# Two-layer graph attention on one core: layer-0 probabilities turned by VectorE in 32x32 blocks over a DRAM scratch, with every engine's order rewritten

## The reference

```python
# layer 0, per graph; H = 8 heads of hd = 64
Q, K, V = x @ W_q + b_q, x @ W_k + b_k, x @ W_v + b_v
scores = einsum('bihd,bjhd->bhij', Q, K) / sqrt(hd)
scores = scores + (x @ w_g[:D])[:, :, None] + (x @ w_g[D:])[:, None, :] + b_g + log(adj + 1e-9)
x1 = einsum('bhij,bjhd->bihd', softmax(scores), V) + x
# layer 1, per graph; one head of 512
q, k = x1 @ Wq + bq, x1 @ Wk + bk
attn = where(adj == 0, 0, softmax(where(adj == 0, -1e18, q @ k.T / sqrt(512))))
out = layernorm(x1 + (attn @ x1) @ Wc) * gamma + beta
```

## Time and profile before

| | |
|---|---|
| median of 3 runs | 2469.9 us (2468.51 to 2470.04) |
| the profiled execution, its own time | 2468.04 us |
| its span, first to last instruction | 2466.3 us |
| share of the span busy | PE 98%, DVE 72%, ACT 52%, POOL 31% |
| DMA | 119.36 MB, 13.5% of 16 engines' span |
| one step | 74.78 us |

### The profile page before, as it was taken

One profiled execution on the slowest core, in us unless ns is written; L12 is line 12 of the kernel. 1 busy time (PEld: TensorE's weight loads), 2 busy tenths in 40 slices (PEclk: granted clock), 3 DMA queues, 4 the chain that ended last, 5 costly groups with the idle time before them and its releaser, 6 DMA issues.

```text
span 2466.3 us, 40779 instructions
## 1 busy us (share of the span) xinstructions
PE 2425.6 (98%) x14544; PEld 2003.8 (81%) x14544; DVE 1777.0 (72%) x5600; ACT 1278.4 (52%) x3602; POOL 774.0 (31%) x1022
## 2 busy tenths in 40 slices
PE   7999999999999999999999999999999999999995
PEld 5888888888888888888888888888888888888884
DVE  4667777767777777777677777687777777776766
ACT  4455445555455555455554455554555554555542
POOL 0133223332323332333332233323233323234322
PEclk9999999999999999999999999999999999999998
DMA  5010111110111101111101111101111111111000
GB/s 197 31 56 22 56 48 47 54 50 29 56 48 44 56 30 48 48 56 44 56 22 56 48 54 46 56 23 56 48 44 56 35 44 52 52 43 57 27 14 26
DMA packets 63179, 119.36 MB, mean 48 GB/s; under 512 B 6272, under 2 KB 22784, under 8 KB 58752
## 3 DMA queue, kind: packets, MB, share of 16 engines
q1 hardware_dynamic: 62976, 116.75, 13.5%
HBM read 83.17 MB, written 33.55 MB: 47 GB/s over the span
## 4 chain that ended last, share of the span: by engine, by line
PE 96%; DVE 1%; SPq 1%; ACT 1%; DMA 0%; issue 0%; POOL 0%; DVEq 0%
PE bank L199 25%; PE bank L201 24%; PE bank L200 24%; PE bank L383 6%; PE bank L404 5%; PE bank L540 5%; PE bank L393 5%; PE bank L319 1%; PE bank L502 1%; PE bank L584 1%; DVE x1n L935 0%; DMA x1n<-in_wkT 0%; ACT probs L680 0%; PE bank L341 0%; PE bank L329 0%
## 5 line engine op out<-in xcount | busy, mean ns | idle before, releaser
L1122 POOL TENSOR_TENSOR probs<-probs,rcp 128x512 f32<-128x512 f32 x256 | 297.3, 1182 | 1105.5 <-DVE rcp L887 1105.5
L680 ACT ACTIVATE probs<-probs,nmax 128x128 f32<-128x128 f32 x1024 | 397.0, 389 | 144.2 <-DVE nmax L877 144.2
L935 DVE STREAM_TRANSPOSE x1n<-x1T 32x512 f32<-32x512 f32 x512 | 359.6, 702 | 8.1 <-DMA out<-x1n 1.6
L877 DVE CUSTOM_DVE_ANT_0 probs<-bank,bias 128x128 f32<-128x128 f32 x1024 | 226.9, 286 | 40.0 <-issue 40.0
L857 DVE TENSOR_TENSOR v_sb<-bank,bv_b 128x512 f32<-128x512 f32 x128 | 87.8, 687 | 229.6 <-PE bank L404 172.9
L706 ACT ACTIVATE g_sb<-bank,consts 128x512 f32<-128x512 f32 x128 | 88.1, 688 | 309.8 <-PE bank L201 308.0
L199 PE MATMUL bank<-x_hi,wk_hi 128*128 128x512 f32 x512 | 209.2, 409 | 8.6 <-DVE x_lo L818 8.6
L199 PE MATMUL bank<-wv_hi,x_hi 128*128 128x512 f32 x512 | 208.6, 407 | 0.4 <-DVE wv_lo L843 0.4
L199 PE MATMUL bank<-x_hi,wm_hi 128*128 128x512 f32 x512 | 204.9, 400 | 3.0 <-DVE x1n L1000 2.4
L199 PE MATMUL bank<-wc_hi,x_hi 128*128 128x512 f32 x512 | 203.5, 397 | 0.0
L199 PE MATMUL bank<-x_hi,wq_hi 128*128 128x512 f32 x512 | 202.7, 396 | 0.0
(11 more groups left out here) (133 smaller groups left out, 5650.7 us busy)
## 6 DMA issues: line engine op xcount, KB each, us to landing
out<-x1n SPq DMA_DIRECT2D x128, 256.0 KB, 2.0
xn<-in_x SPq DMA_DIRECT2D x126, 256.0 KB, 5.0
xT_land<-in_xT SPq DMA_DIRECT2D x31, 1024.0 KB, 5.5
adj_sb<-in_adj SPq DMA_DIRECT2D x32, 256.0 KB, 2.9
v_sb<-in_wk SPq DMA_DIRECT2D x4, 256.0 KB, 5.1
xT_land<-in_xT SPq DMA_DIRECT2D x4, 256.0 KB, 6.1
xT_land<-in_wq SPq DMA_DIRECT2D x4, 256.0 KB, 7.8
probsT<-in_wv SPq DMA_DIRECT2D x4, 256.0 KB, 6.0
```

The costliest lines, as they stand in the source:

```text
L680: op = nc.scalar.activation(probs[:, k, :], probs[:, k, :], ACT.Exp, bias=nmax[:, k:k + 1], scale=-1.0, accum_out=sums[:, k:k + 1])
L877: op = nc.vector.tensor_tensor_reduce(out=probs[:, k, :], in0=bank[4 + h][:, (k % HALF) * P:(k % HALF + 1) * P], in1=bias0[:, k % HALF, :] ...
L935: op = nc.vector.transpose(x1n[b * BLK:(b + 1) * BLK, :, :] .rearrange("p g (c a s) -> p a c g s", c=C, a=P // BLK)[:, a, :, :, :], x1T[a ...
L1122: nc.gpsimd.tensor_tensor(probs[:, half, :], probs[:, half, :], rcp[:, half].unsqueeze(2).to_broadcast([P, HALF, P]), ALU.mult)\
```

## The change

For layer 0's probabilities PE's `turn` and ACT's `turned` are gone. VectorE turns the 8 maps in one instruction of 128x1024, in blocks of 32x32 within each quarter of the partitions (`turn` on DVE, buffer `turned`), and SP moves the blocks to their places: one store of 512 KB to a DRAM scratch, a wait for it, and four loads of 128 KB into a quarter of the partitions of `probsT` each (`move_probs`). `pv` reads `probsT` in a block layout. VectorE's eviction of V moves to ScalarE (`v_out`), its bias is added in `residual0` instead, and the low part of the next x is made by POOL (`next_x_low`) in place of VectorE. The order of all five engines is new: `pv` of head pairs 2 and 3 comes in the next step, after its second `project_q`; the contexts 2 and 3 of layer 1 and the store of its results also come one step later (w = t-2 in the code); the last two `y` products stand at the end of a step.

```diff
-        probsT = [sb(f"probsT{i}", [P, PAIR, P]) for i in range(2)]
+        turned = sb("turned", [P, P // BLK, PAIR, BLK])
+        probsT = [sb(f"probsT{i}", [P, P // BLK, PAIR, BLK]) for i in range(2)]
...
+            def move_probs(t, c):
+
+                sp.wait_ge(s["dve_t"], nth("dve_t", t, c))
+                if c >= 2:
+                    sp.wait_ge(s["pe_pv"], nth("pe_pv", t, c - 2))
+                elif t > 0:
+                    sp.wait_ge(s["pe_pv"], nth("pe_pv", t - 1, c + 2))
+                sp.dma_start(turn_dram[c], turned[:, :, :, :].rearrange("p b k s -> p (b k s)"))\
+                    .then_inc(s_pw[c], 16)
+                sp.wait_ge(s_pw[c], 16 * (t + 1))
+                for b in range(P // BLK):
+                    sp.dma_start(probsT[c % 2][b * BLK:(b + 1) * BLK, :, :, :].rearrange("r a k s -> r a (k s)"),
+                                 turn_dram[c].rearrange("(a r) (b x) -> b r a x", a=P // BLK, b=P // BLK)[b])\
+                        .then_inc(s_pt[c], 16)
+
+            def store(v, g):
+                sp.dma_start(out[bass.ds(v * COLS + g * P, P), :], x1n[:, g, :]).then_inc(s_out[g], 16)
...
-            def turn(t, c):
-
-                for h in range(2):
-                    pe.wait_ge(s["pool_p"], nth("pool_p", t, 2 * c + h))
-                    for k in range(HALF):
-                        mm = nc.tensor.transpose(bank[6 + h][:, k * P:(k + 1) * P],
-                                                 probs[:, h * HALF + k, :], ident[:, :])
-                    mm.then_inc(s["pe_t"], 1)
-
-            def pv(t, c, b):
-
-                pe.wait_ge(s["act_pt"], nth("act_pt", t, 2 * c + 1))
+            def pv(t, c):
+
+                pe.wait_ge(s_pt[c], 16 * PT_MOVES * (t + 1))
                 if c == 0:
-                    pe.wait_ge(s["dve_v"], nth("dve_v", t, GG - 1))
+                    pe.wait_ge(s["act_v"], nth("act_v", t, GG - 1))
+                b = pv_bank(c)
                 for g in range(GG):
                     for e in range(2):
-                        mm = nc.tensor.matmul(bank[b][e * HD:(e + 1) * HD, g * P:(g + 1) * P],
+                        mm = nc.tensor.matmul(b[e * HD:(e + 1) * HD, g * P:(g + 1) * P],
                                               v_sb[:, g, c * P + e * HD:c * P + (e + 1) * HD],
-                                              probsT[c % 2][:, e * GG + g, :], start=True, stop=True)
+                                              probsT[c % 2][:, :, e * GG + g, :], start=True, stop=True)
...
+            def context_rest(w):
+
+                pe.wait_ge(s["dve_pv"], nth("dve_pv", w + 1, 1))
+                context(w, 2)
+                pe.wait_ge(s["dve_res"], nth("dve_res", w, 1))
+                context(w, 3)
...
+                if w >= 0:
+                    pe.wait_ge(s["dve_y"], nth("dve_y", w, 3))
...
+                project_k(t, 0)
+                if w >= 0:
+                    context_rest(w)
+                    pe.wait_ge(s["dve_tp"], nth("dve_tp", w))
...
+                gate_rows(t)
...
+                project_q(t, 0)
...
+                project_v(t, 0)
+                scores(t, 0)
+                if w >= 0:
+                    pe.wait_ge(s["dve_res"], nth("dve_res", w, 3))
+                project_v(t, 1)
+                project_k(t, 1)
+                project_q(t, 1)
+                if w >= 0:
+                    pe.wait_ge(s["dve_res"], nth("dve_res", w, 2))
+                else:
+                    pe.wait_ge(s["dve_pv"], nth("dve_pv", u, 1))
+                pv(u, 2)
+                pe.wait_ge(s["dve_b"], nth("dve_b", t))
+                pv(u, 3)
                 scores(t, 1)
...
                 project_k(t, 2)
...
+                project_v(t, 2)
+                project_v(t, 3)
+                gw(0)
+                gw(1)
+                pe.wait_ge(s["dve_pv"], nth("dve_pv", u, 3))
+                pair_scores(u, 0, False)
+                gw(2)
+                pair_scores(u, 1, False)
+                gw(3)
+                pair_scores(u, 2, False)
+                pair_scores(u, 3, False)
                 project_q(t, 2)
-                if first:
-                    pe.wait_ge(s["dve_v"], nth("dve_v", t, 3))
-                    m_chunk(2)
-                pe.wait_ge(s["act_pt"], nth("act_pt", t, 1))
-                turn(t, 1)
...
+                pe.wait_ge(s["dve_pv"], nth("dve_pv", u, 2))
+                pv(t, 0)
                 scores(t, 2)
...
+                yw(0)
+                yw(1)
                 project_k(t, 3)
+                pe.wait_ge(s["dve_sa"], nth("dve_sa", u))
+                turn_attention(u, False)
                 project_q(t, 3)
...
                 pe.wait_ge(s["dve_pv"], nth("dve_pv", t, 0))
-                pe.wait_ge(s["dve_pv"], nth("dve_pv", t, 1))
-                turn(t, 2)
-                if not first:
-                    cx(3)
+                pv(t, 1)
                 scores(t, 3)
-                if first:
-                    m_columns()
-                pv(t, 2, 6)
+                pe.wait_ge(s["dve_tp"], nth("dve_tp", u))
+                context(u, 0)
+                context(u, 1)
+                yw(2)
+                yw(3)
...
-            def turned(t, c):
-
-                for h in range(2):
-                    act.wait_ge(s["pe_t"], nth("pe_t", t, 2 * c + h))
-                    nc.scalar.activation(probsT[c % 2][:, h * HALF:(h + 1) * HALF, :]
-                                         .rearrange("p a b -> p (a b)"),
-                                         bank[6 + h][:, :], ACT.Copy).then_inc(s["act_pt"], 1)
+            def v_out(t, g):
+                act.wait_ge(s["pe_v"], nth("pe_v", t, g))
+                nc.scalar.activation(v_sb[:, g, :], bank[2 + g % 2][:, :], ACT.Copy).then_inc(s["act_v"], 1)
...
+            def next_x_high(it):
+                act.wait_ge(s["pe_q"], nth("pe_q", it.t, C - 1))
+                act.wait_ge(s_xT[1 - it.par], 16 * (it.p + 1))
+                for c in range(C):
+                    x_hi_chunk(1 - it.par, c)
...
-            def v_out(t, g):
-                dve.wait_ge(s["pe_v"], nth("pe_v", t, g))
-                nc.vector.tensor_tensor(v_sb[:, g, :], bank[2 + g % 2][:, :], bv_b[:, :], ALU.add)\
-                  .then_inc(s["dve_v"], 1)
...
-            def residual0(t, c, b, par):
+            def turn(t, c):
+
+                dve.wait_ge(s["pool_p"], nth("pool_p", t, 2 * c + 1))
+                if c > 0:
+                    dve.wait_ge(s_pt[c - 1], 16 * PT_MOVES * (t + 1))
+                elif t > 0:
+                    dve.wait_ge(s_pt[C - 1], 16 * PT_MOVES * t)
+                nc.vector.transpose(turned[:, :, :, :],
+                                    probs[:, :, :].rearrange("p k (b r) -> p b k r", b=P // BLK))\
+                  .then_inc(s["dve_t"], 1)
+
+            def residual0(t, c):
 
                 dve.wait_ge(s["pe_pv"], nth("pe_pv", t, c))
-                nc.vector.tensor_tensor(x1T[:, c, :], bank[b][:, :], xT_land[par][:, c, :], ALU.add)\
-                  .then_inc(s["dve_pv"], 1)
+                nc.vector.scalar_tensor_tensor(out=x1T[:, c, :], in0=pv_bank(c)[:, :],
+                                               scalar=bv0_c[:, c:c + 1], in1=xT_land[t % 2][:, c, :],
+                                               op0=ALU.add, op1=ALU.add).then_inc(s["dve_pv"], 1)
 
...
+                turn(u, 3)
+                if w >= 0:
+                    residual1(w, 2)
+                bias(t)
+                if w >= 0:
+                    residual1(w, 3)
+                x1lo(u, 0)
+                x1lo(u, 1)
+                maxima(t, 0)
...
+                    next_gate(t + 1, 0)
+                    next_gate(t + 1, 1)
+                recips(t, 0)
+                residual0(u, 2)
+                residual0(u, 3)
+                turn(t, 0)
+                maxima(t, 1)
+                x1lo(u, 2)
+                x1lo(u, 3)
+                x1_rows(u, 0)
+                recips(t, 1)
+                x1_rows(u, 1)
+                turn(t, 1)
+                row_terms(u, False)
+                masked_scores(u, False)
+                residual0(t, 0)
+                attention1(u)
+                maxima(t, 2)
+                y_low(u, 0, False)
+                recips(t, 2)
+                y_low(u, 1, False)
...
+                    next_gate(t + 1, 2)
+                turn(t, 2)
+                att1T_low(u, False)
+                maxima(t, 3)
+                residual0(t, 1)
...
+                    next_gate(t + 1, 3)
+                y_low(u, 2, False)
+                residual1(u, 0)
+                y_low(u, 3, False)
+                residual1(u, 1)
+                recips(t, 3)
...
+            def next_x_low(t):
+
+                for c in range(C):
+                    pool.wait_ge(s["act_x"], nth("act_x", t + 1, c))
+                    nc.gpsimd.tensor_tensor(x_lo[:, c, :], xT_land[(t + 1) % 2][:, c, :],
```

(54 more changed lines are left out.)

943 lines of the change are left out of this document (448 added, 495 removed).

## The result

The changed kernel takes 2407.9 us (median of 4 runs, 2407.2 to 2408.9) against 2470.0: ratio 0.975, 95% interval 0.9733 to 0.9767. The forecast was 2418, with a range of its own of 2405 to 2432.

What follows compares the result with a forecast made beforehand. PE was taken as the bound, busy 98% of the span. Turns -107.5, fourth-y wait +48, `pair_scores` +3 and last step +5 gave -51.5: span 2414.8, median 2418 us; range 2370 to 2458, the forecast's own 2405 to 2432.

Steps and rivals of the forecast that it cites:

- turns off PE: On PE, four turns per step over 32 steps, 128 at 0.84 us each, come off its list: -107.5 us.
- wait for the fourth y: `project_k` directly behind the last `yw` on bank 1 makes PE wait 1.6 us in 30 places: +48 us.
- four `pv`: On PE, `pv` reading its operand in pieces of 32 columns: taken 0, bounds nothing to 58 us.
- `pair_scores`: Fourth `pair_scores` behind the third waits for ACT's copy of `gw(3)`: 0.1 us a step taken, bounds 0 and 0.2, +3 us.
- What bounds the kernel: PE, busy 98% of the span and all 74.78 us of a step; a new wait on it adds in full.
- rival (e): `pv` in blocks costs more: a quarter to all of its 58 us, 2433 to 2476; chance 0.03.
- The last step: Layer 1 alone: PE idles 8.6 us before its first products; +3.3 of chain and 2 of lower clock, +5 us taken.
- The cover: Before the first context about 2.3 us left; round trip 9 us (about 6 to 11.8) against 15 for head pair 3.
- Rival (b): A chain of DVE and POOL is late: PE waits 1 to 1.5 us more a step, 2449 to 2465; chance 0.24.
- Rival (c): VectorE's turn takes its four quarters in sequence, 5.6 us: kernel about 2780, sign turning near 5.4; chance 0.04.
- row of 0.58: Old trace's granted clock of 0.58 over 6.10 us after an idle stretch; priced up to 2.6 us, 2 taken, last step.
- 0.11 for slower: Chance of a slower kernel: dear VectorE turn, long round trip, and the worst of late chains and dearer `pv`.

## Why the prediction came out so

Direction and mechanism were right; the time was 10 us high, the span 7.7. By its own terms, a step:

| term | forecast | measured |
|---|---|---|
| turns off PE | -3.36 | -3.34 (0.87 + 0.79 + 0.89 + 0.79 in one step of before) |
| wait for the fourth y | +1.6 | +1.57 |
| four `pv` | 0 | -0.17 (four of 1.03; now 1.90 for two, 1.02, 1.02) |
| `pair_scores` | +0.1 | -0.05 (0.81 + 0.81 + 0.99 + 0.91; now 0.81, 0.81, 1.85 for two) |
| other | 0 | +0.03 |
| step | 73.1 | 72.81 |

*What bounds the kernel:* right. PE's list plus one wait gives the step to 0.03 us.

*The turns* and *the wait* were the two large terms, and each was then measured by itself: 106.3 against 107.5 (with a new wait in the 106.3, see there), and 52 for the wait with its slow starts against 48. The wait's parts were right as well: ACT starts 0.19 behind the last matmul's slot and DVE 0.03 behind ACT. VectorE came free 0.30 us before ACT's copy was done.

*`pv` and `pair_scores`* were mis-sized by 0.32 a step together, 10 us in 30 steps, which is more than the whole miss in the span; the ends took 1.3 of it back. I gave `pv` in pieces of 32 columns an upper bound of 58 us (rival (e)): it costs nothing, 1.02 against 1.03. But the 0.45 us from which that bound was worked out was wrong: a `pv` takes 1.02 already before the change, where the trace has 16 matmuls for its 8. Twice as long would have been some 130 us more and slower than before, so the rival's range ended too low by more than half; that nothing was added owes nothing to that sum. Two small groups in a row save a little: the second `pv` starts 0.88 us behind the first, where another group starts 1.02 behind it.

*The last step:* PE idle 8.2 us, forecast 8.6. Behind it the clock was 0.50 and 12 matmuls took 5.29 us (2349.79 to 2355.08) in place of 2.72, 2.6 more, where I took 2. The wait for the attention fell from 10.2 to 6.9, where I took 3.1 off. The ends together (the two steps of 32 that are not full) changed by -0.4 us, where the sum had -1.7.

*The cover:* the turn at 1.24 was cheaper than taken, and a trip took 7.3 us and not 9; both were hidden, as argued. But 7.3 is the median of all; head pair 0 takes 11.0 and up to 12.5, beyond my upper end of 11.8, with cover enough. For the loads the estimate by the Trainium skill ("SBUF — State Buffer", § Door 1 for the rate, § The DMA setup-cost knee for the fixed 2), 0.7 us for 128 KB behind a fixed 2, fits the 2.8 measured to landing; for four in turn it gives 4.8 us, and from the first issue to the last landing the median is 4.4. The low parts of x on POOL took 1.40 each instead of 1.2, and beside them the gate's second pass took 1.77 us. With POOL's block gone it took 0.68. The Trainium skill ("SBUF — State Buffer", § SBUF: two separate sides) has VectorE operations with two SBUF inputs and POOL's operations exclude each other; these two rows agree with it.

*Where the reasoning failed, though the number did not.* Three rivals were priced by "each us of wait is 30 us". This step held for the 0.18 more of one needless product and was wrong from 0.65 more on. Rival (b), a late chain, was given 2449 to 2465 for 1 to 1.5 us more; 0.65 more at the y already gave 2482, above that range and above the kernel before. Rival (c) was to turn the sign when a turn costs 5.4 us: at 5.0 the kernel takes 2645. What failed there is the granted clock, which I had priced for the last step alone, from the row of 0.58, and the cover, which I had read for one turn at a time (2.3) where several stand ahead of the same wait on one queue. The changed kernel, with 1.41 us idle in each step, was nearer to a loss than my 0.11 for slower says: 0.65 us more idle at that place takes all of the gain.

## What to carry to other kernels

Where one engine is busy all the time, add up its list by the spacing of groups, and for every new neighbourhood of two products ask which bank they share and who reads it out: this table of banks held 52 us, nearly as much as the whole change gave. A wait on TensorE has two prices: its length and, from some length on and then nearly each time, the clock behind it; so read how far each remaining wait is from the next row at which the clock fell. Cover is a matter of a queue: what each of several repeated instructions adds can count once for each that stands ahead of the wait.
